# Transformer kernel: the residual's modulated rows made by GpSimd in token layout in place of TensorE identity products

## What is computed

```python
emb = silu(_sin_emb(timestep)) @ W_ada + b_ada          # one row of 512 per entry
scale, shift = split(emb[:, None, :], 2, axis=-1)
x = _ln(src) * (1.0 + scale) + shift                     # the modulated rows
q, k, v = x @ Wq + bq, x @ Wk + bk, x @ Wv + bv          # 16 heads of 16
probs = softmax(where(src_mask, -inf, q @ k.T / 4 + attention_bias))
x = x + (probs @ v) @ Wo + bo                            # the residual in question
h = _ln(x) * g2 + beta2
return x + gelu2(h @ W1 + b1) @ W2 + b2
```

## Time and profile before

| | us |
|---|---|
| median of three runs | 1383.22 |
| the profiled execution, its own time | 1381.58 |
| its span | 1379.8 |
| PE busy | 1254.1 (91%) |
| DVE busy | 987.8 (72%) |
| ACT busy | 904.7 (66%) |
| POOL busy | 665.7 (48%) |
| granted TensorE clock, mean | 0.976 |

### The profile page before, as it was taken

The page is one execution under the profiler, slowest core; times in us unless marked ns, Lnnn a source line. Parts: engine busy times, 40 slices in busy tenths (PEclk is TensorE's granted clock), DMA queues, the critical chain, the costliest instruction groups (busy, mean ns, idle before and its releaser), DMA issues.

```text
span 1379.8 us, 34480 instructions
## 1 busy us (share of the span) xinstructions
PE 1254.1 (91%) x9923; PEld 1156.6 (84%) x9923; DVE 987.8 (72%) x2764; ACT 904.7 (66%) x2319; POOL 665.7 (48%) x580
## 2 busy tenths in 40 slices
PE   4886799999999999993789999999999999999996
PEld 4775699999999999992568888888888888888885
DVE  5777687798888879754387767677677777776652
ACT  3442677787778778751557776777767777667671
POOL 2776377787787778773113232332323323231222
PEclk9999999999999999996789999999999999999998
DMA  5885122211111211204966676666766667665620
GB/s 181 272 281 196 60 58 59 58 48 48 58 58 58 58 58 57 59 32 153 283 214 205 211 213 202 201 199 201 233 190 199 194 199 234 191 201 166 214 70 16
DMA packets 184708, 203.18 MB, mean 147 GB/s; under 512 B 18177, under 2 KB 172737, under 8 KB 184577
## 3 DMA queue, kind: packets, MB, share of 16 engines
q1 hardware_dynamic: 169136, 161.57, 38.2%
q10 hardware_dynamic: 9264, 23.47, 5.3%
q0 software_dynamic: 6176, 16.79, 3.5%
HBM read 155.89 MB, written 41.68 MB: 143 GB/s over the span
## 4 chain that ended last, share of the span: by engine, by line
PE 44%; issue 3%; ACT 3%; DVE 2%; DMA 1%; ACTq 1%; POOL 0%; POOLq 0%; DVEq 0%
PE ps_p L1361 8%; PE ps_s L1347 4%; PE ps_ctx L1377 4%; PE ps_s L1349 4%; PE ps_out L1475 3%; PE ps_q L1475 3%; PE ps_q L1428 2%; PE ps_q L1461 2%; PE ps_k L1461 2%; PE ps_k L1428 2%; PE ps_out L1418 2%; PE ps_q L1436 2%; ACT bias L1254 2%; PE ps_out L1398 1%; PE ps_q L1465 1%
## 5 line engine op out<-in xcount | busy, mean ns | idle before, releaser
L1254 ACT ACTIVATE bias<-bias,neg_max 128x256 f32<-128x256 f32 x512 | 255.0, 500 | 84.2 <-DVE neg_max L1584 83.5
L343 POOL TENSOR_TENSOR w_lo<-w,w_hi 128x512 fp32r<-128x512 f32 x156 | 241.6, 1569 | 0.0
L1584 DVE CUSTOM_DVE_ANT_0 bias<-ps_s,bias 128x256 f32<-128x256 f32 x512 | 194.4, 417 | 33.6 <-PE ps_s L1349 19.8
L745 DVE TENSOR_TENSOR w_lo<-w,w_hi 128x512 fp32r<-128x512 f32 x156 | 149.2, 995 | 72.1 <-ACT w_hi L423 70.4
L544 PE MATMUL ps_y<-w_hi,hidT_hi 128*128 128x256 f32 x624 | 180.4, 289 | 3.5 <-DVE token_rows L759 3.5
L531 PE MATMUL ps_h<-htokT_hi,w_hi 128*128 128x256 f32 x624 | 178.0, 285 | 3.2 <-DVE htokT_lo L750 3.2
L531 PE MATMUL ps_h<-htokT_lo,w_hi 128*128 128x256 f32 x624 | 177.6, 285 | 0.0
L531 PE MATMUL ps_h<-htokT_hi,w_lo 128*128 128x256 f32 x624 | 177.6, 285 | 0.0
L544 PE MATMUL ps_y<-w_lo,hidT_hi 128*128 128x256 f32 x624 | 177.1, 284 | 0.0
L544 PE MATMUL ps_y<-w_hi,hidT_lo 128*128 128x256 f32 x624 | 177.0, 284 | 0.0
L1198 POOL TENSOR_TENSOR act_lo<-up_f,act_hi 128x512 fp32r<-128x512 f32 x64 | 82.7, 1292 | 184.4 <-ACT act_hi L1301 184.4
(11 more groups left out here) (276 smaller groups left out, 3570.8 us busy)
## 6 DMA issues: line engine op xcount, KB each, us to landing
bias<-bias_dram SPq DMA_DIRECT2D x128, 512.0 KB, 4.2
w<-w_dram ACTq DMA_DIRECT2D x32, 512.0 KB, 5.2
xin<-dispatch SPq DMA_DIRECT2D x39, 256.0 KB, 2.7
expert_out<-token_rows SPq DMA_DIRECT2D x39, 256.0 KB, 2.2
q_stack<-q_hi_rows SPq DMA_DIRECT2D x64, 128.0 KB, 2.9
q_stack<-q_lo_rows SPq DMA_DIRECT2D x64, 128.0 KB, 2.9
k_stack<-k_hi_rows SPq DMA_DIRECT2D x60, 128.0 KB, 2.9
k_stack<-k_lo_rows SPq DMA_DIRECT2D x60, 128.0 KB, 2.8
```

The costliest lines, as they stand in the source:

```text
L343: pool.tensor_tensor(w2_part["lo"][:, k, :], w2_piece(e, k), w2_part["hi"][:, k, :].bitcast(F32), ALU.subtract).then_inc(sem("w2_split"), 1)
L745: dve.tensor_tensor(w1_part["lo"][:, k, :], w1_piece(e, k), w1_part["hi"][:, k, :].bitcast(F32), ALU.subtract).then_inc(sem("w1_split"), 1)
L1254: act.activation(head_rows(h, j), head_rows(h, j), ACT.Exp, scale=-1.0, bias=neg_max[par][:, h, j:j + 1], accum_out=total[par][:, h, j:j + ...
L1584: dve.tensor_tensor_reduce(head_rows(h, j), ps_s[h % 2][:, j * T:(j + 1) * T], head_rows(h, j), -1.0, LARGEST, ALU.add, ALU.min, neg_max[p ...
```

## The change

The modulated rows are made a second time, in token layout, by GpSimd: xn (still in token layout, the normalised input) times a row of 1 + scale, plus a row of shift + bo, both rows broadcast over the partitions. Two operations of 128x512 do it (`keep_rows`, now on GpSimd). The rows of all entries are made once in the first stage: two more products on TensorE (16x512 output), three more operations on VectorE, and a DMA to DRAM (`mod_rows`). SP then loads one entry's row with a broadcasting DMA of 256 KB (`load_mod`), in the place in its queue where the copy of xmT stood; it no longer waits for the output product there. `residual` adds the new rows in place of bo. The identity products are gone. GpSimd now waits for h_rows, the second normalised rows, before x3b, so that x3b, the two new operations and the mask all come behind them. VectorE's `normalise` of entry n+2 waits until GpSimd has read xn.

```diff
         sp.dma_start(b1[:], io["b1"]).then_inc(sem("b1_in"), 16)
+        sp.dma_start(cond["ada_row"], io["ada_row"].partition_broadcast(B)).then_inc(sem("ada_rows_in"), 16)
+        sp.dma_start(cond["bo_row"], io["rows"][1].partition_broadcast(B)).then_inc(sem("ada_rows_in"), 16)
         for b in range(2, B):
+            if b == 8:
+                sp.wait_ge(sem("mod_rows_ready"), 2)
+                sp.dma_start(io["mod_rows"], cond["rows"]).then_inc(sem("mod_sent"), 16)
...
             if b == 14:
                 act.wait_ge(sem("cond_product"), 6)
+                act.wait_ge(sem("mod_sent"), 16)
...
+    for c in range(C):
+        pe.matmul(ps_a[0:B, 0:2 * D], w["wave"][:, c, :], w["ada_w"][:, c, :], start=(c == 0), stop=(c == C - 1))
     for m in range(2 * C):
...
     dve.wait_ge(sem("cond_product"), 6)
+    dve.wait_ge(sem("ada_rows_in"), 32)
+    dve.tensor_tensor(w["rows"], ps_a[0:B, 0:2 * D], w["ada_row"], ALU.add).then_inc(sem("rows_summed"), 1)
...
+    dve.wait_ge(sem("rows_summed"), 1)
+    dve.tensor_scalar(w["rows"][:, 0:D], w["rows"][:, 0:D], 1.0, None, ALU.add).then_inc(sem("mod_rows_ready"), 1)
+    dve.tensor_tensor(w["rows"][:, D:2 * D], w["rows"][:, D:2 * D], w["bo_row"], ALU.add).then_inc(sem("mod_rows_ready"), 1)
...
-        def keep_rows(n, par):
-
-            sp.wait_ge(sem("xmT_ready"), C * (n + 1))
-            wait_free(sp, sem("wo_done"), n - 1, alone=True)
-            sp.dma_start(xmT_kept[par][:], xmT[:]).then_inc(sem("xm_kept"), 16)
+        def load_mod(n):
+
+            wait_free(sp, sem("xm_rows_ready"), n, alone=True)
+            sp.dma_start(mod_rows[:].rearrange("p i d -> p (i d)"), io["mod_rows"][bass.ds(n, 1), :].rearrange("b d -> (b d)").partition_broadcast(P)
+                         ).then_inc(sem("mod_in"), 16)
...
+        def keep_rows(n, par):
+
+            pool.wait_ge(sem("xn2_ready"), J * (n + 1))
+            pool.wait_ge(sem("mod_in"), 16 * (n + 1))
+            pool.tensor_tensor(xm_rows[par][:], xn[:], spread(mod_rows[:, 0, :], [P, J, D], 1), ALU.mult).then_inc(sem("xm_scaled"), 1)
+            wait_alone(pool, sem("xm_scaled"), n + 1)
+            pool.tensor_tensor(xm_rows[par][:], xm_rows[par][:], spread(mod_rows[:, 1, :], [P, J, D], 1), ALU.add).then_inc(sem("xm_rows_ready"), 1)
...
                 rsqrt(rstd2, mv2, "var2_ready", "rstd2_ready", n - 1)
+                pool.wait_ge(sem("h_rows_ready"), J * n)
                 prepare_sum(n - 1)
             if exists(n + 1):
+                keep_rows(n + 1, 1 - par)
                 take_mask(n + 1, 1 - par)
...
             wait_free(act, sem("v_done"), n)
-            wait_free(act, sem("xm_kept"), 16 * n)
...
             pe.wait_ge(sem("ctxT_ready"), n + 1)
-            pe.wait_ge(sem("xm_kept"), 16 * (n + 1))
             for j in range(J):
                 for m in range(C):
                     sums = ps_out[:, j * D + m * P:j * D + (m + 1) * P]
                     for c in range(C):
-                        pe.matmul(sums, ctxT[:, c, j * P:(j + 1) * P], wo[:, c, m * P:(m + 1) * P], start=(c == 0), stop=False)
-                    last = pe.matmul(sums, xmT_kept[par][:, m, j * P:(j + 1) * P], ident, start=False, stop=True)
+                        last = pe.matmul(sums, ctxT[:, c, j * P:(j + 1) * P], wo[:, c, m * P:(m + 1) * P], start=(c == 0), stop=(c == C - 1))
...
             dve.wait_ge(sem("rstd_ready"), n + 1)
+            wait_free(dve, sem("xm_rows_ready"), n)
...
             dve.wait_ge(sem("wo_done"), n + 1)
+            dve.wait_ge(sem("xm_rows_ready"), n + 1)
...
-            dve.tensor_tensor(x3[:], halves(ps_out[:, :]), spread(bo[:], [P, J, D], 1), ALU.add).then_inc(sem("x3_ready"), 1)
+            dve.tensor_tensor(x3[:], halves(ps_out[:, :]), xm_rows[par][:], ALU.add).then_inc(sem("x3_ready"), 1)
```

More of the change, by code:

```diff
@@ L505, in _ @@
             if b == 3:
-                wave_tensor(pe, cond, ps_h1, sem)
+                wave_tensor(pe, cond, ps_h0, ps_h1, sem)
             step(b)
@@ L828, in cond_weights @@
         "hyp_w1": place(SE, 1536, SH), "hyp_w2": place(SH, 1664, SH), "sty_w1": place(SH, 1792, SH // 2),
+        "rows": more[0:B, 512:1024], "ada_row": more[0:B, 1024:1536], "bo_row": more[0:B, 1536:1792],
         "a1": sb("a1", [SH, B]), "a2": sb("a2", [SH, B]), "a3": sb("a3", [SH // 2, B]),
@@ L852, in style_tensor, with wave_tensor @@
     last.then_inc(sem("cond_product"), 1)
-def wave_tensor(pe, w, ps_b, sem):
+def wave_tensor(pe, w, ps_a, ps_b, sem):
     pe.wait_ge(sem("wave_ready"), 1)
     pe.wait_ge(sem("ada_in"), 16)
+    for c in range(C):
+        pe.matmul(ps_a[0:B, 0:2 * D], w["wave"][:, c, :], w["ada_w"][:, c, :], start=(c == 0), stop=(c == C - 1))
     for m in range(2 * C):
@@ L1010, in transformer @@
     w2 = {n: sb(f"ff2_{n}", [P, F, D], F32R) for n in ("hi", "lo")}
-    bv, bo, b2 = [sb(n, [P, D]) for n in ("bv", "bo", "b2")]
+    bv, b2 = [sb(n, [P, D]) for n in ("bv", "b2")]
     q_b = sb("q_b", [P, C])
@@ L1023, in transformer @@
     xmT = sb("xmT", [P, C, T])
-    xmT_kept = [sb(f"xmT_kept{i}", [P, C, T]) for i in range(2)]
+    mod_rows = sb("mod_rows", [P, 2, D])
+    xm_rows = [sb(f"xm_rows{i}", [P, J, D]) for i in range(2)]
     part = {n: sb(n, [P, C, T], F32R) for n in ("q_hi", "q_lo", "k_hi", "k_lo")}
@@ L1240, in load_layer @@
                 act.dma_start(dst, io["ff_b1"][i * 512:(i + 1) * 512].partition_broadcast(P)).then_inc(sem("fold_in"), 16)
-            for i, dst in enumerate((bo, b2)):
-                act.dma_start(dst[:], io["rows"][1 + i].partition_broadcast(P)).then_inc(sem("layer_in"), 16)
+            act.dma_start(b2[:], io["rows"][2].partition_broadcast(P)).then_inc(sem("layer_in"), 16)
             act.dma_start(wo[:], io["wo"]).then_inc(sem("layer_in"), 16)
@@ L1408, in turn_x, with output @@
             last.then_inc(sem("xnT2_done"), 1)
-        def output(n, par):
+        def output(n):
             pe.wait_ge(sem("ctxT_ready"), n + 1)
-            pe.wait_ge(sem("xm_kept"), 16 * (n + 1))
             for j in range(J):
@@ L1512, in step @@
                     if h == 3:
-                        output(n - 1, 1 - par)
+                        output(n - 1)
                 if exists(n + 1):
@@ L1625, in take_values, with residual @@
                                   bv[:].rearrange("p (m i w) -> p m i w", m=GROUPS, w=HD), ALU.add).then_inc(sem("v_ready"), 1)
-        def residual(n):
+        def residual(n, par):
             dve.wait_ge(sem("wo_done"), n + 1)
+            dve.wait_ge(sem("xm_rows_ready"), n + 1)
             wait_free(dve, sem("h_rows_ready"), J * n)
             wait_free(dve, sem("x3b_ready"), n)
-            dve.tensor_tensor(x3[:], halves(ps_out[:, :]), spread(bo[:], [P, J, D], 1), ALU.add).then_inc(sem("x3_ready"), 1)
+            dve.tensor_tensor(x3[:], halves(ps_out[:, :]), xm_rows[par][:], ALU.add).then_inc(sem("x3_ready"), 1)
         def moments(n):
@@ L1755, in step @@
                     if h == 4:
-                        residual(n - 1)
+                        residual(n - 1, 1 - par)
                         moments(n - 1)
@@ L1878 @@
         "ff_w1": chunks(second("W1")), "ff_w2": chunks(second("W2")),
-        "ff_b1": second("b1"),
+        "ff_b1": second("b1"), "ada_row": second("b_ada"),
         "rows": np.stack([second("bv"), second("bo"), second("b2")]),
```

9 lines of the change are left out of this document (5 added, 4 removed).

## The result

The changed kernel takes 1370.1 us (median of four runs, 1368.73 to 1371.74) beside 1382.83 us for the kernel before on the same chip (1380.78 to 1383.97). The ratio is 0.9908, 95% interval 0.9895 to 0.9920: 12.7 us faster. The forecast was 1371.0, in a range of 1362 to 1378.

A forecast was written before the change was run, and what follows sets the result against it. TensorE was taken to set the pace, with some 1.3 us idle per entry. From 1381.58 us, -13.2 - 2.2 + 3.1 = -12.3 gives 1369.3; the median being 1.64 higher, 1371, range 1362 to 1378.

The forecast's parts named there:

- The identity products, -13.2 us: TensorE, place 3: removing four pairs saves 0.88 us per entry, in 15 entries 13.2 us.
- h_rows worth nothing in the entries: VectorE: h_rows falls from 1.99 to 0.73 us behind GpSimd's new order, yet the steady gain is 0.
- rival D: Something other than x3b holds h_rows at 1.99; only the tail's 0.9 us moves, inside the forecast, no separate chance.
- Rival A: TensorE's gaps at places 6 and 7 close: 15 us more, about 1356, or half, about 1363; chance 0.12.
- signs of being wrong: Minima or v_pad lengthen, act_lo waits for its own queue, or TensorE's idle time per entry exceeds 1.3 us.
- The tail, -2.2 us: Last entry, not covered by other work: h_rows gives -0.9 us and the identity products 1.3.
- GpSimd hidden, VectorE not held: GpSimd's 5.3 us stretch behind h_rows leaves 3.8 us before act_lo and holds no VectorE operation: cost 0.
- rival C: GpSimd's two new operations each hold a VectorE operation by 1.27 us: slower, about 1390 to 1408; chance 0.09.
- The first stage, +3.1 us: Round b = 3: TensorE's new products add 1.72 us and VectorE's three operations 1.4, nothing hiding them.
- four such take 1.72 us: First stage, round b = 3: TensorE's price for the four instructions of the two new products with 512 columns.
- The upper bound of 4: First stage: the added cost lies between 0, if later rounds absorb it, and 4 us, with waits.
- The sum: Whole kernel: -13.2 - 2.2 + 3.1 = -12.3 us.

The follow-up runs named there:

- e1: The kernel before with the identity products left out, copy of xmT and x3b's place kept: ratio 0.9888 to the kernel before, 15.5 us faster.
- e2: The kernel before with one wait more, so that GpSimd starts x3b only behind h_rows: ratio 0.9996 to the kernel before.
- e7: The changed kernel with turn_h moved ahead of the scores and transposes of place 6 on TensorE: ratio 0.9801 to the kernel before.
- e5: The kernel before, run once more unchanged for its trace: ratio 0.9995 to the kernel before.
- e3: The kernel before with only the first stage's additions (rows made, summed, sent to DRAM, read by nothing): ratio 1.0020 to the kernel before.
- e11: The changed kernel with the first of GpSimd's two row operations done three times over: ratio 0.9908 to the kernel before.
- e4: The changed kernel without GpSimd's wait for h_rows: ratio 0.9930 to the kernel before.

## Why the prediction was right, step by step

**The identity products, -13.2 us.** Right. A piece group fell from 2.60 to 1.71, place 3 from 3.59 to 2.72 on average, and e1 alone gives 15.5 us with the tail.

**h_rows worth nothing in the entries.** Right, both in its length (0.74 for 1.99, so rival D is out) and in its price: e2 shows no change. The reason given, the chain turn_h, hT_hi, exponentials of head 7, is shown by e7, where starting that chain earlier takes 0.95 us out of an entry. Rival A named the same gap, but the change didn't touch what it hangs on.

One of the prediction's signs of being wrong did come up: TensorE's idle time in the steady window is 1.73 us, above its bound of 1.3. It was a poor sign. The gap at place 6 reads 1.26 where the two before made 1.04, but place 6 takes 2.76 us in both traces, and place 3 gave its whole 0.87. Ends of matmuls are modelled, and the widths of the places decide.

**The tail, -2.2 us.** It came out at about twice that by the traces, and the rest beyond the two parts was luck of TensorE's clock. h_rows gave 0.94. The rest is told by the windows over the output product of the last entry in four traces: before, e5 (before again), the changed kernel, and e3, which has the identity products too (columns as above, PEclk is the third number from the end).

```profile
1350.00:1355.00 5.00, 4.64 (x24) 4.45 (x24) 0.26 (x2) 0.00 (x0) 0.00 (x0) 0.61 0.01 3
```

```profile
1354.30:1360.00 5.70, 5.49 (x24) 5.19 (x24) 0.12 (x2) 0.00 (x0) 0.00 (x0) 0.50 0.01 3
```

```profile
1342.00:1345.00 3.00, 2.05 (x16) 1.86 (x16) 0.86 (x2) 0.00 (x0) 0.00 (x0) 1.00 0.00 0
```

```profile
1359.50:1362.50 3.00, 2.92 (x24) 2.75 (x24) 0.02 (x1) 0.00 (x0) 0.00 (x0) 1.00 0.02 5
```

At the lower level the 24 products take 5.5 us, at 1.00 they take 2.9, with nothing changed in them. From the 14th h_rows to the last e5 has 76.81 us and e3 74.27, though their tails are the same code: 2.5 us come and go with the clock, and the changed kernel's trace had it at 1.00. Its other three runs have no trace, so how much of this stands in the median is open.

**GpSimd hidden, VectorE not held.** Right in the steady entries: 3.72 us are left in front of act_lo (3.8 forecast), the load of the rows lands in 4.3 us (3 to 4 forecast), v_pad, minima and residual keep their lengths, and e11 makes the stretch 2.8 us longer for nothing.

In one place rival C's mechanism did occur, and the prediction had not looked there: entry 0 of the transformer, where VectorE prepares weights (a small operation from SBUF, 0.60 us in the trace of before) while GpSimd makes the rows of entry 1. DVE and POOL of the changed kernel:

```profile
685.20 2.37 DVE L1706 TENSOR_SCALAR h_rows<-const,vec 128x128 f32<-128x128 f32 x2
```

```profile
684.84 1.28 POOL L1226 TENSOR_TENSOR xm_rows<-xn,mod_rows 128x512 f32<-128x512 f32 x1 [11.88 <-DMA mod_rows<-mod_rows_dram]
686.20 1.29 POOL L1228 TENSOR_TENSOR xm_rows<-xm_rows,mod_rows 128x512 f32<-128x512 f32 x1
```

It is held until the second row operation ends, the minimum behind it is late, and place 7 takes 2.30 us in place of 1.35. Place 7 of entry 0 is 2.11 to 2.39 in all eight traces with the new rows and 1.35 or 1.36 in all six without: 0.8 to 1.0 us, which the sum did not have. GpSimd's operations fall there because it waits 11.88 us for the load of the rows.

**The first stage, +3.1 us.** The mechanism was right and the size was not: the trace gives 4.6 where the first expert product starts. VectorE's part was 1.1 against 1.4. TensorE's was 3.5 against 1.7, for the four instructions in this trace and in e11's alike. The step that failed is "four such take 1.72 us": I took a product's price from the transformer for a stage in which TensorE works at half of that pace. The trace of before could have told it, for in front of the products of the earlier trace rows, which start at 31.48, stand four transposes of 128x128 that take 0.22 us each, where the transformer's take 0.09 to 0.11:

```profile
30.59 1.09 PE L498 MATMUL ps_y<-const,columns 128*128 128x128 f32 x4
```

The upper bound of 4, which I had set for waits, doesn't hold the 4.6 either. That the price goes with the stage's pace and not with the product shows in e11, whose TensorE went to the faster pace right behind the same products:

```profile
31.69 3.56 PE L867 MATMUL ps_h<-w,wave 128*16 128x512 f32 x4
35.18 1.96 PE L870 MATMUL ps_h<-wave,w 128*128 128x16 f32 x16
36.99 0.37 PE L478 MATMUL ps_h<-picked,const 128*128 128x16 f32 x2
```

The 16 small products take 1.81 us from start to start, against 3.43 in the traces of the changed kernel, e3, e4 and e7, and the first stage ends 2.2 us earlier, 2.5 later than before. By their mean clock most runs went this way, so the forecast of 3.1 lies between the two courses, for a reason that it did not have: the new products cost twice their price, and TensorE's pace behind them often gives some of it back.

**The sum** came out in part because errors cancelled, and that is luck. The trace's span gives -11.4 us against the -12.3 of the forecast. The forecast had 1.5 us too little for the first stage, 1.7 for entry 0 (0.9 at place 7, and 0.9 at place 15 less 0.3 at place 0; e2 and e5, without the new rows, have the longer place 15 too), and 1.2 in entries 1 to 13, where the late ctxT took 1.4 (mean place 2 at 2.75 against 2.64). Against them stand 2.4 us in the last two entries and the tail, nearly all of it the clock's, and 1.0 in the experts' stage, from the first expert product to the transformer's first transposes, where the fourteen traces lie between 519.4 and 522.3 us with the same code.

## What to carry to other kernels

A product that adds what another engine can add costs TensorE its full time wherever TensorE is the bound, and two broadcast operations in another engine's idle stretch are a fair trade: look for the length of that stretch up to the next instruction that something waits for. An engine made faster off the path is worth nothing until the step on the path that it now allows is moved up; ask at once which instruction may start earlier and move it. Take the price of an instruction from the stage in which it will run, with a neighbour of known size beside it. And hold the traced run against the others: here its mean granted clock was that of one run in four.

## What the runs showed of the hardware

- TensorE at half pace while the granted clock reads 1.00. Over 31 to 38 us in the changed kernel's trace the granted clock is 1.00 and TensorE is busy throughout:

```profile
31.00:38.00 7.00, 7.00 (x21) 3.60 (x20) 2.75 (x21) 1.78 (x4) 4.17 (x4) 1.00 0.95 348
```

  Yet the products there take twice what the same shapes take in the transformer, the pace of 1.2 and not of 2.4 GHz. TensorE had been busy for 13.6 of the 31 us until then. In e11, after 13.2 of 31 us, it changed to the double pace behind the new products and fell back after 38.5 us; there the reading is 0.50 at the same half pace (61.50 us, above) that reads 1.00 in the other traces. In the traces of the changed kernel, e3, e4 and e7, with the same code there, it did not change. So at the start of a trace the reading alone does not tell the pace; the distance between starts does.
- A held VectorE operation was held until GpSimd's ended, and two of GpSimd's in a row held two pieces: h_rows took 0.73, 1.99 and 2.66 us beside none, one and two, and two small operations of entry 0 took 2.37 in place of 0.60. v_pad and the minima, with one input from PSUM, kept their lengths in all runs. The Trainium skill states both sides in SBUF — State Buffer, section Who interferes with whom: a VectorE instruction in a 2-port mode and a GpSimd one block each other fully, and one with at most one SBUF input outside these modes does not contend. The runs agree, as far as lengths can show it; no run shows in which mode h_rows ran.
- The same program has a copy that starts 1.7 to 2.4 us late in ten of its entries in one trace (e5) and on time in another (before), some 5 us in all. A comparison of times on one chip took it out here (0.9995 for e5); a comparison of two traces does not.
